# Attention with a gated low-rank branch on one core: the q/k writes of half the slots on another DMA queue, a low part on another engine, three orders changed

## What is computed

```python
xn = _layernorm(x)
q, k, v = (xn @ Wq.T, xn @ Wk.T, xn @ Wv.T)          # 32, 8, 8 heads of 128
q, k = _rmsnorm(q, q_norm_w), _rmsnorm(k, k_norm_w)
scores = einsum('bkgqd,bksd->bkgqs', qg, k) / sqrt(128)
bias = where(rel > 0, -1e30, slopes * rel)           # rel = key position - query position
attn = softmax(scores + bias)
s = (attn @ v) @ Wo.T
router = 8 * softmax(xn @ Wr.T + br)
g = silu(2 * einsum('bshr,hor,bsh->bso', xn @ A.T, B, router))
y = x + s * g
```

## Time and profile before

| | before |
|---|---|
| median of three runs | 747.57 us |
| the profiled execution | 749.58 us |
| its span | 747.8 us |
| TensorE busy | 722.3 us (97%) |
| VectorE busy | 606.2 us (81%) |
| ScalarE busy | 561.2 us (75%) |
| GpSimd busy | 347.8 us (47%) |
| granted TensorE clock | full in all 40 slices |

### The profile page before, as it was taken

One profiled execution on the slowest core, in us unless ns is written; L12 is line 12 of the kernel. 1 busy time (PEld: TensorE's weight loads), 2 busy tenths in 40 slices (PEclk: granted clock), 3 DMA queues, 4 the chain that ended last, 5 costly groups with the idle time before them and its releaser, 6 DMA issues.

```text
span 747.8 us, 14622 instructions
## 1 busy us (share of the span) xinstructions
PE 722.3 (97%) x3741; PEld 605.6 (81%) x3741; DVE 606.2 (81%) x1482; ACT 561.2 (75%) x1440; POOL 347.8 (47%) x328
## 2 busy tenths in 40 slices
PE   8898999999999999999999999999999999999987
PEld 7787878877888878888788788888788887888777
DVE  7868888688886888687986889878886979868996
ACT  4567778686877877777886878778787768869882
POOL 4224344454434553545444544346436444445656
PEclk9999999999999999999999999999999999999999
DMA  8016958677695878858686776958778685867761
GB/s 302 1 29 160 286 154 236 188 218 221 167 266 158 224 205 221 246 153 257 173 232 197 225 225 169 275 151 230 204 223 233 163 279 153 225 197 207 203 189 71
DMA packets 214773, 148.02 MB, mean 198 GB/s; under 512 B 48992, under 2 KB 205536, under 8 KB 214624
## 3 DMA queue, kind: packets, MB, share of 16 engines
q1 hardware_dynamic: 180192, 128.10, 58.9%
q10 hardware_dynamic: 34560, 19.68, 10.5%
HBM read 85.84 MB, written 61.87 MB: 198 GB/s over the span
## 4 chain that ended last, share of the span: by engine, by line
PE 47%; issue 15%; DVE 15%; POOL 9%; ACT 6%; DMA 6%; SPq 1%; ACTq 1%; DVEq 1%; POOLq 0%
POOL pt_lo L580 5%; PE out_ps L1355 4%; PE out_ps L1357 4%; PE out_ps L1356 4%; PE qkv_ps L1355 4%; PE qkv_ps L1356 4%; PE qkv_ps L1357 4%; PE score_ps L1355 4%; PE score_ps L1357 3%; PE score_ps L1356 3%; POOL inv_rms L570 3%; PE mix_ps L1355 2%; DMA qk_moved<-turning_qk 2%; PE mix_ps L1357 2%; PE mix_ps L1356 2%
## 5 line engine op out<-in xcount | busy, mean ns | idle before, releaser
L580 POOL TENSOR_TENSOR pt_lo<-x_sb,pt_hi 128x512 fp32r<-128x512 f32 x137 | 176.1, 1310 | 257.3 <-ACT pt_hi L786 257.3
L711 ACT ACTIVATE probs<-probs,neg_max 128x128 f32<-128x128 f32 (+3 forms) x256 | 142.1, 559 | 39.9 <-DVE neg_max L1009 38.8
L1009 DVE CUSTOM_DVE_ANT_0 probs<-score_ps,cst,slope 128x128 f32<-128x128 f32 (+3 forms) x256 | 131.2, 543 | 28.0 <-PE score_ps L1357 27.5
L719 ACT ACTIVATE probs<-probs,recip 128x128 f32<-128x128 f32 (+3 forms) x252 | 126.2, 549 | 8.2 <-DVE recip L1016 8.2
L1355 PE MATMUL qkv_ps<-w_hi,xt_hi 128*128 128x256 f32 (+1 forms) x392 | 125.9, 321 | 2.4 <-DVE xt_lo L952 1.4
L1356 PE MATMUL qkv_ps<-w_lo,xt_hi 128*128 128x256 f32 (+1 forms) x392 | 125.7, 321 | 0.0
L1357 PE MATMUL qkv_ps<-w_hi,xt_lo 128*128 128x256 f32 (+1 forms) x392 | 125.2, 319 | 0.0
L786 ACT ACTIVATE pt_hi<-x_sb 128x512 fp32r<-128x512 f32 x153 | 86.6, 625 | 44.8 <-issue 30.5
L570 POOL TENSOR_TENSOR inv_rms<-sums,minus_half 128x5 f32<-128x5 f32 x64 | 78.7, 1230 | 57.9 <-DVE sums L1068 57.9
L1355 PE MATMUL out_ps<-wo_hi,o_hi 128*128 128x512 f32 x252 | 102.5, 407 | 2.3 <-DVE o_lo L1054 2.3
L1030 DVE STREAM_TRANSPOSE squared<-probs 128x256 f32<-128x256 f32 (+3 forms) x124 | 101.7, 821 | 0.3 <-ACT probs L719 0.3
(11 more groups left out here) (191 smaller groups left out, 1597.1 us busy)
## 6 DMA issues: line engine op xcount, KB each, us to landing
turning_qk<-qk_squared ACTq DMA_DIRECT2D x240, 80.0 KB, 2.0
qk_moved<-turning_qk SPq DMA_DIRECT2D x60, 320.0 KB, 3.3
turning<-squared SPq DMA_DIRECT2D x120, 128.0 KB, 2.3
x_sb<-turning SPq DMA_DIRECT2D x30, 512.0 KB, 5.0
w_raw<-wqkv SPq DMA_DIRECT2D x32, 384.0 KB, 5.2
turning<-squared SPq DMA_DIRECT2D x120, 96.0 KB, 2.0
x_sb<-turning SPq DMA_DIRECT2D x30, 384.0 KB, 4.2
turning<-squared SPq DMA_DIRECT2D x128, 64.0 KB, 1.8
```

The source lines that it names most:

```text
L580: nc.gpsimd.tensor_tensor(by_quad(pt_lo, j), moved_block(t, j), by_quad(pt_hi, j).bitcast(F32), ALU.subtract).then_inc(pt_lo_by_pool, 1)
L711: nc.scalar.activation(probs[:, h, 0:n], probs[:, h, 0:n], ACT.Exp, bias=neg_max[:, h:h + 1], scale=-1.0, accum_out=total[:, h:h + 1]).the ...
L719: nc.scalar.activation(to[:, h, 0:n], probs[:, h, 0:n], ACT.Copy, scale=recip[:, h:h + 1]).then_inc(probs_ready, 1)
L1009: nc.vector.tensor_tensor_reduce(probs[:, h, 0:n], score_bank(t, h), cst[:, C_DIST + SEQ - n:C_DIST + SEQ], slope[:, h:h + 1], HUGE, ALU.a ...
```

## The change

Five things change.

1. `BY_POOL` goes from 2 to 1: of block 3's four low parts GpSimd makes one and VectorE three (before, two each), in all eight groups.
2. In the loop's slots 4, 5, 0 and 1, those of one or two key blocks, the four writes of q and k of unit t + 2 are issued by SP at the beginning of its `move`, ahead of the probabilities' writes, and no longer by ScalarE. In slots 3, 6, 7 and 2, in the start and in the last group ScalarE issues them as before.
3. At the start, SP reads q and k of block 3 between the two pairs of writes of block 1's probabilities.
4. At the start, VectorE squares block 1's probabilities after it has normalized and squared q and k of block 3.
5. In the last group's end, VectorE's fourth bias of block 6 comes ahead of an `add_out`, and gates 4 and 5 come behind block 6's low parts and the second reciprocals of block 7.

```diff
--- before.py
+++ after.py
@@ -69,7 +69,7 @@


 W_SLOT = 5
-BY_POOL = 2
+BY_POOL = 1

 WO_POOL, WO_DVE = (0, 1, 3), 2

@@ -402,6 +402,10 @@
         def is_last(t, left):
             return left == 1 and t == BLOCKS - 1

+        def written_by_sp(g, t):
+
+            return keys_of(t) <= 2 and not (isinstance(g, int) and g == GROUPS - 1) and t > 1
+
         def last_turns(t):

             return sum(keys_of(u) for u in range(BY_PE, t))
@@ -457,6 +461,11 @@

                 i, to = t % QB, moved[t % 2]
                 n = (i + 1) * P // 2
+                if u is not None and written_by_sp(g, t):
+                    sp.wait_ge(qk_squared_ready, ONE(g, u - BY_TURN, 1))
+                    for q in range(QUADS):
+                        sp.dma_start(turning_qk[u % 2, q, :, :].rearrange("(k r) n -> r k n", k=QUADS),
+                                     qk_squared[q * QUAD:(q + 1) * QUAD, :, :]).then_inc(qk_written, 16)
                 write_probs(g, t, 0)
                 if soon:
                     sp.wait_ge(qk_lo_ready, K_AND_Q_LO(g, u, 0))
@@ -519,7 +528,7 @@

             sp.wait_ge(xt_turned, BLOCKS)
             move(0, 0, None)
-            move(0, 1, BY_TURN)
+            move(0, 1, BY_TURN, True)
             slot(0, 2, GROUPS)
             pipeline(sp, slot)
             for t in range(BLOCKS - 2):
@@ -824,7 +833,7 @@
                     split_wo(g + t // BLOCKS, range(0, HPG))
                 if here(t - 2, left):
                     mixed_hi(g, t - 2, left)
-                if by_squares(t + 2, left) and not wo_due:
+                if by_squares(t + 2, left) and not wo_due and not written_by_sp(g, t):
                     write_qk(g, t + 2)
                 if here(t - 1, left) and not by_both(t - 1):
                     moved_hi(g, t - 1)
@@ -1229,8 +1238,8 @@
                     bias(g, before, h, singly=True)
                 turned_qk_lo(g, last, True)
                 reciprocals(g, before, 0)
+                bias(g, before, 3, singly=True)
                 add_out(g, before - 3)
-                bias(g, before, 3, singly=True)
                 multiply_gate(range(2, 4))
                 mixed_lo(g, before - 2, 1)
                 reciprocals(g, before, 2)
@@ -1238,12 +1247,12 @@
                     bias(g, last, h, at_end=True)
                 add_out(g, before - 2)
                 bias(g, last, 3, at_end=True)
-                multiply_gate(range(4, 6))
                 mixed_lo(g, before - 1, 1)
                 reciprocals(g, last, 0)
                 for n in range(keys_of(before)):
                     turned_lo(before, n)
                 reciprocals(g, last, 2)
+                multiply_gate(range(4, 6))
                 add_out(g, before - 1)
                 multiply_gate(range(6, BLOCKS))
                 mixed_lo(g, before, 1)
@@ -1337,11 +1346,11 @@
             square_sums(0, 3)
             value_lo(0, 3)
             turned_low_lo(3)
-            square_probs(0, 1, 0)
-            square_probs(0, 1, 2)
             normalize_k(0, 3)
             normalize_q(0, 3)
             square_both(0, 3)
+            square_probs(0, 1, 0)
+            square_probs(0, 1, 2)
             dve.wait_ge(acc_ready, 1)
             slot(0, 2, GROUPS)
             pipeline(dve, slot)
```

## The result

In 20 runs of each kernel beside one another the changed kernel takes 750.55 us and the kernel before 746.91: a ratio of 1.0048, 95% interval 1.0036 to 1.0060. That is 3.6 us more (2.7 to 4.5), where 1.3 were forecast. The profiled execution after took 750.40 us (span 748.6), near its median; the one of before (749.58) is 2.7 us above the median of its 20 runs. One execution of a later kernel (after_not5) took 1171.8 us, far outside all others, and is left out of its comparison.

What follows compares the result with a forecast made beforehand. TensorE's saturated stretch plus a chain through ScalarE, GpSimd, VectorE, DMA and slot 5 bound each pass. Terms +1.75 + 0 - 0.35 + 0.4 - 0.4 - 0.1 = +1.3 us gave 748.9 us on 747.57; range 743.0 to 753.0.

Steps and rivals of the forecast that it cites:

- What bounds the kernel: A loop pass is TensorE's saturated 42.2 us, then a 44.5 us chain ending in slot 5, pt_hi to k_lo 11.0.
- The q/k writes: Slot 1: SP's queue slides 0.69 us, delaying block 3's landing 0.25 us a pass; +1.75 us in seven, 0 to +4.8.
- 0.34 us behind q_hi, as in slot 4: Slot 1's chain: ScalarE's next issue can follow q_hi by 0.34 us, so it comes 0.25 us later.
- Value of the freed time: nothing.: Loop slots 0, 1, 4, 5: ScalarE's 16 dropped issues a pass gain 0, since pt_hi waits for a landing.
- One low part by GpSimd: Block 3's low parts: 0 in seven passes; in the last group -0.35 us, from -0.8 to +0.3.
- The start: Kernel's start: block 1's second half is written 2.3 us later, part arriving at slot 5; +0.4 us, -1.25 to +1.5.
- The end: Last group: moved gates -0.4 us (-1.8 to +0.6), block 6's fourth bias ahead of add_out -0.1.
- One heir: Last group: the 1.81 us wait for o_lo goes, but later gates delay the next o_lo, already waited for 0.52 us.
- The slide in full: Slot 1, q_hi of block 3: the whole 0.69 us shows each pass, +4.8 us, 752.0 in all; chance 0.18.
- The sooner landing of block 3: Block 3's read ahead of slot 5 lands up to 0.94 us a pass sooner, 741.0 or 744.3 us; chance 0.22.
- rule of turns between the queues: DMA engines alternate between queues with work, so ScalarE's q/k writes would share engines with the read ending at slot 5's start.
- The signs: Expected in the trace: pt_hi to k_lo 11.0 us, twelve SP issues in slot 1, q/k read near 326.7, 1.81 wait moved.

Runs made afterwards that it cites:

- after_not5: The changed kernel, but ScalarE again issues the q and k writes in slot 5; 748.80 us against 747.18 of the kernel before, ratio 1.0031 (1.0006 to 1.0057).
- p1: The kernel before with only BY_POOL going from 2 to 1 (GpSimd makes one low part of block 3, VectorE three); ratio 0.9998 (0.9980 to 1.0017).

## Why the prediction was right in its sign and small in its size

The sign was right and the time, 750.55 us, lies in the range of 743.0 to 753.0. That is in part luck: 1.3 us were forecast and 3.6 measured. Of these, 1.6 come from a collision that no term had, and 1.2 lie in a stretch to which the prediction gave nothing. The base was high as well: 747.57 is the median of the first three runs, and all 20 have 746.91.

**What bounds the kernel.** Right: from pt_hi to k_lo slot 5 is 10.96 to 11.15 us in 80 of the 84 passes behind the first that the 14 profiles have, and up to 11.55 in the other four, whatever the low parts did. Incomplete: the prediction called the stretch from block 6 to block 2 TensorE's, for its 42.19 of 42.20 us. Block 7's probabilities bind there just as block 3's do: from their pt_hi in slot 1 to k_lo of block 2 it is 11.04 to 11.08 us in every pass of every kernel, and in six of before's seven passes the scores of block 2 follow this k_lo by 0.13 to 0.23. A full TensorE had a second chain right behind it.

**The q/k writes: +1.75 forecast.** The mechanism was right to its last step, the size was not. 0.69 us of slide on SP (0.72 measured), q_hi 0.69 later (0.59), ScalarE's issue 0.25 later (0.06), the read of block 3 0.25 later (0.10 +- 0.07): 0.7 us in seven passes. The step that failed is "0.34 us behind q_hi, as in slot 4": in slot 1 the issue can follow q_hi by 0.14. The price came from one row of another slot, the nearest that there was, and it was 0.2 us too long: that is most of what 0.25 was made of.

**"Value of the freed time: nothing."** This failed twice. In slot 4 it took the 0.28 us of ScalarE's own delay ahead of pt_hi away; the landing came later by half of that, and no gain can be told. In slot 5 it was worth less than nothing: +0.23 us a pass, 1.6 us, the largest term of the change that is shown, and in no line of the sum. The prediction asked what the freed engine would gain and stopped at the landing; it did not ask whom the sooner pt_hi would set off, and beside whom that one would run. The rows for it were in the trace of before: GpSimd waiting for ScalarE's pt_hi, and a copy 0.11 us ahead of it.

**One low part by GpSimd: 0 in the loop, -0.35 in the last group.** Right in the loop. In the last group the 0.66 us wait went and one of 0.37 for o_lo came; from pt_hi to the end it is 41.90 in p1 against 42.09 in before, -0.2 in one pair, where equal code varies by 1.2.

**The start: +0.4.** About right (+0.3 +- 0.3), with a slide of 2.5 us on pt_hi where 1.15 was taken and less of it that arrived.

**The end: -0.5.** Together with the last group's -0.35 the forecast was -0.85; the profiles give -0.6 +- 0.2 for the two, and -0.4 +- 0.3 without the clock. So the sign was right and the size is not told from the forecast. One heir was named, o_lo behind gates 6 and 7 (a wait of 1.15 us where 0.52 was). The other, 0.84 us for the last o_lo, was not: it came by way of GpSimd, which waits for gate 4.

**The read of block 7: no term.** The prediction left slots 0 and 1 without a price in the saturated stretch, for want of idle time there. With SP's writes the stretch from block 7 to block 2 takes 1.2 +- 0.3 us more in seven passes; this is measured, and its cause is open.

**Sum of what was measured:** 0.7 + 1.6 - 0.6 + 0.3 + 1.2 = 3.2 us, of 3.6 (2.7 to 4.5). Only the 1.6 has its cause shown by edits that undo it; each of the others has an uncertainty of 0.2 to 0.5, so that the sum comes this near is no proof of them.

**The rivals.** The slide in full (752.0) did not happen: q_hi slid by 0.59 of the 0.69 us, the issue behind it by 0.06. The sooner landing of block 3 (741 to 744) did not either: with slot 4's writes on SP's queue it takes 6.99 us against 6.84, not 0.94 less. The Trainium skill's rule of turns between the queues, which the prediction had weighed for this rival (DMA: Bandwidth & Descriptors, "Queues, rings and completion order"), would have had it sooner; the traces don't agree with it here, before or after. Before, the first packet of ScalarE's four writes starts 0.82 us behind the first issue where no such read is out, and 2.1 to 3.5 us behind it in all 14 slots 4 and 0 of the loop, in which the read of block 3 or 7 is. In the pass of the earlier trace rows the issue is at 352.92, the first packet at 356.29, and pt_hi behind the landing starts at 356.63. These writes stood behind the read already, so SP's queue had nothing to take out of its way.

**The signs.** pt_hi to k_lo, SP's twelve issues, the read at 326.7 and the growth of the 18.0 us stretch (0.2 +- 0.07 on a mean of 49 passes a side, 0.14 by the medians, 0.2 to 0.3 foretold) came as said. The 1.81 us wait left one of 1.14 and one of 0.81 behind it.

## What to carry to other kernels

Follow freed time to its end: list who waits for the engine that is freed, let each start sooner, and look at what it will then run beside. A copy of five columns just ahead of a bias for which TensorE waits cost 0.23 us a pass here, and taking four DMA issues off another engine in that slot gained nothing. Take the size of a small term from all profiles that share the code in question: one pair gave 0.0 us for the end, 14 profiles give -0.6. And a distance that is the same to 0.02 us in all passes of one kernel and 0.2 different in all passes of the other finds such a cause in one pair of profiles, when their whole spans differ by chance more than by the change.

## What the runs showed of the hardware

VectorE's copy of 128 x 5 fp32 values takes 0.13 to 0.16 us, and 0.93 when GpSimd's tensor_tensor of 128 x 512 (1.29 us) has begun 0.39 us ahead of it; before the change it was 0.13 in all seven passes of the loop (the greatest of the row is that at the start):

```profile
L994 DVE COPY factor<-cst x8: 126/128/166, 15.6 to 628.8; 128x5 f32 x7, 128x5 f32<-128x5 f32 x1
```

Executions differ by places where no edit acts. The first score product stands at 28.1 to 31.1 us in the 14 profiles, ahead of every edit: 3 us, nearly as much as the whole result. The spread is there when TensorE transposes the second block of x (10.4 to 13.4 us), after the first at 5.8 to 7.7. In the six profiles in which the second came later than 11.3 us, the granted clock was 1.2 GHz for a stretch between 7.7 and 14.5 us; in the other eight there is none. A DMA issue of usually 0.45 us took over 0.9 us 5 to 13 times in an execution, in all kernels. Between its issue and its landing, the read of 1 MB of transposed probabilities of a block with four key blocks, in two DMAs, took from 5.6 to 8.9 us.
